# Each 1024-column scan run as two of 512 columns, one per channel block

## What is computed

```python
delta = softplus(dlt @ W_dt.T + b_dt)                       # (L, 1024)
A = -exp(A_log)                                             # (1024, 16)
deltaA = exp(delta[..., None] * A)
deltaBx = delta[..., None] * Bm[:, :, None, :] * xc[..., None]
def step(h, inp):                                           # over the positions
    dA, dBx, c = inp
    h = dA * h + dBx
    return (h, einsum('bdn,bn->bd', h, c))
y = (ys + xc * D) * silu(z)
out = y @ W_out.T
```

## Time and profile before

| what | value |
|---|---|
| median of 3 runs | 5346.54 us |
| lowest and highest | 5343.88 and 5351.52 us |
| span of the profiled execution | 5344.5 us |
| first scan to last scan | 136.8 to 3693.0 us |
| feed-forward part | from about 3700 us |
| DVE, PE, POOL, ACT busy over the span | 91%, 90%, 73%, 66% |

### The profile page before, as it was taken

One profiled execution on the slowest core, in us unless ns is written; L12 is line 12 of the kernel. 1 busy time (PEld: TensorE's weight loads), 2 busy tenths in 40 slices (PEclk: granted clock), 3 DMA queues, 4 the chain that ended last, 5 costly groups with the idle time before them and its releaser, 6 DMA issues. The chain is left out here.

```text
span 5344.5 us, 78097 instructions
## 1 busy us (share of the span) xinstructions
PE 4819.1 (90%) x21964; PEld 3313.7 (62%) x21964; DVE 4883.6 (91%) x4117; ACT 3542.1 (66%) x7757; POOL 3924.5 (73%) x1818
## 2 busy tenths in 40 slices
PE   8789898898988988889898898877999999999999
PEld 3455555555555555555555555555788888888888
DVE  7999999999999999999999999997788888888887
ACT  3777878778788787877877778765444444444442
POOL 5999999999999999999999999997222322223221
PEclk9899999999999999999999999988999999999999
DMA  7555565655555555555555555555001010110100
GB/s 249 173 187 186 179 197 175 190 190 173 192 177 194 190 172 192 179 188 183 185 190 175 192 184 180 184 167 185 27 31 33 29 35 29 31 33 29 35 29 28
DMA packets 402710, 745.76 MB, mean 140 GB/s; under 512 B 44083, under 2 KB 44211, under 8 KB 402198
## 3 DMA queue, kind: packets, MB, share of 16 engines
q1 hardware_dynamic: 401590, 738.08, 42.4%
q0 software_dynamic: 736, 3.41, 0.2%
HBM read 698.05 MB, written 43.26 MB: 139 GB/s over the span
## 5 line engine op out<-in xcount | busy, mean ns | idle before, releaser
L739 POOL TENSOR_TENSOR slot<-du,b_row 128x1024 f32<-128x1024 f32 x1024 | 2396.3, 2363 | 23.6 <-issue 15.5
L1119 DVE TENSOR_TENSOR_SCAN decays<-decays,state,slot 128x1024 f32<-128x1024 f32 x656 | 1539.0, 2346 | 59.1 <-ACT slot L970 58.3
L961 ACT ACTIVATE decays<-delta,rate 128x512 f32<-128x512 f32 x2048 | 1326.9, 679 | 23.8
L1250 PEld LDWEIGHTS y_ps<-ident,slot 128*128 128x128 f32 x8192 | 969.9, 146 | 336.5 <-issue 221.3
L1250 PE MATMUL y_ps<-ident,slot 128*128 128x128 f32 x8192 | 1058.2, 281 | 101.0 <-POOL slot L746 76.4
L1175 PE MATMUL work_ps<-h_t,win 128*128 128x512 f32 x2048 | 962.9, 614 | 83.9 <-ACT zs L839 34.7
L746 POOL TENSOR_TENSOR slot<-slot,c_row 128x1024 f32<-128x1024 f32 x368 | 868.6, 2360 | 131.6 <-ACT state L948 125.4
L1640 POOL TENSOR_TENSOR hq<-hid,qinv 128x1408 f32<-128x1408 f32 x63 | 163.3, 2593 | 1029.9 <-DVE qinv L1666 1029.9
L1119 DVE TENSOR_TENSOR_SCAN slot<-decays,state,slot 128x1024 f32<-128x1024 f32 x368 | 857.2, 2339 | 26.0 <-ACT slot L970 25.9
L1125 DVE TENSOR_TENSOR slot<-decays,c_row 128x1024 f32<-128x1024 f32 x656 | 801.9, 1222 | 54.5 <-DVE decays L1119 0.5
L1175 PEld LDWEIGHTS work_ps<-h_t,win 128*128 128x128 f32 x2048 | 385.9, 196 | 531.8 <-issue 431.2
(11 more groups left out here) (283 smaller groups left out, 7980.9 us busy)
## 6 DMA issues: line engine op xcount, KB each, us to landing
b_row<-b_c_rows SPq DMA_DIRECT2D x1024, 256.0 KB, 3.9
c_row<-b_c_rows SPq DMA_DIRECT2D x1024, 256.0 KB, 3.7
win<-in_w_in SPq DMA_DIRECT2D x256, 256.0 KB, 4.3
xt<-in_x SPq DMA_DIRECT2D x16, 1024.0 KB, 7.4
xr<-in_x SPq DMA_DIRECT2D x64, 256.0 KB, 4.1
x_after_mamba<-xr SPq DMA_DIRECT2D x64, 256.0 KB, 4.3
xa<-x_after_mamba SPq DMA_DIRECT2D x64, 256.0 KB, 2.8
xres<-x_after_mamba SPq DMA_DIRECT2D x64, 256.0 KB, 2.7
```

The lines of the kernel that those rows point to most:

```text
L739: pool.tensor_tensor(slot[:, u % SLOTS, :, :], du[:, p % 2, :, :], two(b_row[:, u % BC_RING, :]), ALU.mult).then_inc(S["ub_ready"], 1)
L961: act.activation(decay[u % 2][:, i, :], delta[:, p % 2, i, :], ACT.Exp, scale=rate[:, 2 * p + i, n:n + 1]).then_inc(S["decay_ready"], 1)
L1119: dve.tensor_tensor_scan(d if u in DVE_C else h, d, h, state[:, 2 * p, n:n + 1], ALU.mult, ALU.add).then_inc(S["scan_done"], 1)
L1250: op = pe.matmul(y_ps[i][:, s, :], slot[:, u % SLOTS, i, s * P:(s + 1) * P], ident[:, :], is_transpose=True, start=False, stop=(n == N - 1 ...
```

## The change

The scan, the C product on VectorE, the decays and the saving of states go by half units (one channel block each); the seam steps (`lead_exp`, `lead_mul`, `lead_in`) and their three buffers and five semaphores are gone. 41 units stay in `DVE_C`, but some are others: 1, 10, 16, 48 and 57 leave, 3, 15, 49, 55 and 58 come in. The step tables and `BANK` are new, with most steps moved by a position or two. GpSimd's B and C products stay 1024 wide. The diff, with the tables cut:

```diff
-                    def save_states(u, c):
+                    def save_state(u, i, c):
                         p, n = divmod(u, N)
-                        h = decay[u % 2] if u in DVE_C else slot[:, u % SLOTS, :, :]
                         if u in DVE_C:
-                            wait(act, *c_done(u, c))
-                        else:
-                            wait(act, S["scan_done"], c.at(UNITS, u + 1))
-                        act.activation(state[:, 2 * p:2 * p + 2, n], h[:, :, T - 1], ACT.Copy).then_inc(S["state_saved"], 1)
+                            wait(act, *((S["half_used"], half_used(u, c)) if i == 0 else c_done(u, c)))
+                            act.activation(state[:, 2 * p + i, n:n + 1], decay[u % 2][:, i, T - 1:T], ACT.Copy).then_inc(S["state_saved"], 1)
+                        elif i == 0:
+                            wait(act, S["scan_done"], c.at(2 * UNITS, 2 * u + 2))
+                            act.activation(state[:, 2 * p:2 * p + 2, n], slot[:, u % SLOTS, :, T - 1], ACT.Copy).then_inc(S["state_saved"], 2)
...
+                    def decays(u, i, c):
...
                         if n == 0:
-                            wait(act, *piece_read("d", 2 * p + 1, c))
-                            wait(act, S["lead_cut"], c.at(PAIRS, p + 1))
+                            wait(act, *piece_read("d", 2 * p + i, c))
                         if exists(cc) and v in DVE_C:
-                            wait(act, S["state_saved"], c.at(UNITS, u - 1))
-                        for i in (1, 0):
-                            act.activation(decay[u % 2][:, i, :], delta[:, p % 2, i, :], ACT.Exp,
-                                           scale=rate[:, 2 * p + i, n:n + 1]).then_inc(S["decay_ready"], 1)
-                    def lead_in(u, c):
-                        p, n = divmod(u, N)
-                        first = slot[:, u % SLOTS, 1, 0:1]
-                        if n == 0:
-                            wait(act, S["lead_ready"], c.at(PAIRS, p + 1))
-                        wait(act, S["ub_ready"], c.at(UNITS, u + 1))
-                        act.activation(first, first, ACT.Identity, bias=lead[:, p % 2, n:n + 1]).then_inc(S["u_led"], 1)
+                            wait(act, S["state_saved"], c.at(2 * UNITS, 2 * (u - 2) + i + 1))
+                        act.activation(decay[u % 2][:, i, :], delta[:, p % 2, i, :], ACT.Exp,
+                                       scale=rate[:, 2 * p + i, n:n + 1]).then_inc(S["decay_ready"], 1)
...
-                    def scan(u, c):
+                    def scan(u, i, c):
...
-                        wait(dve, S["decay_ready"], c.at(2 * UNITS, 2 * u + 2))
-                        wait(dve, S["u_led"], c.at(UNITS, u + 1))
-                        d, h = flat(decay[u % 2][:, :, :]), flat(slot[:, u % SLOTS, :, :])
-                        dve.tensor_tensor_scan(d if u in DVE_C else h, d, h, state[:, 2 * p, n:n + 1],
+                        wait(dve, S["decay_ready"], c.at(2 * UNITS, 2 * u + i + 1))
+                        if i == 0:
+                            wait(dve, S["ub_ready"], c.at(UNITS, u + 1))
+                        d, h = decay[u % 2][:, i, :], slot[:, u % SLOTS, i, :]
+                        dve.tensor_tensor_scan(d if u in DVE_C else h, d, h, state[:, 2 * p + i, n:n + 1],
                                                ALU.mult, ALU.add).then_inc(S["scan_done"], 1)
-                    def times_c(u, c):
-                        wait(dve, *ring_loaded(c_loaded, c, u))
-                        wait(dve, S["scan_done"], c.at(UNITS, u + 1))
-                        dve.tensor_tensor(slot[:, u % SLOTS, :, :], decay[u % 2][:, :, :], two(c_row[:, u % BC_RING, :]),
-                                          ALU.mult).then_inc(c_row_used[u % BC_RING], 1)
+                    def times_c(u, i, c):
+                        if i == 0:
+                            wait(dve, *ring_loaded(c_loaded, c, u))
+                        wait(dve, S["scan_done"], c.at(2 * UNITS, 2 * u + i + 1))
+                        op = dve.tensor_tensor(slot[:, u % SLOTS, i, :], decay[u % 2][:, i, :], c_row[:, u % BC_RING, :], ALU.mult)
...
-                                scan(pos, c)
+                                scan(pos, 0, c)
+                                scan(pos, 1, c)
...
-                                times_c(pos, c)
+                                times_c(pos, 0, c)
+                                times_c(pos, 1, c)
```

More of the change, by code:

```diff
@@ L32 @@
 BANK = {
[7 rows of a table removed]
[6 rows of a table added]
 }
 PE_STEPS = {
[11 rows of a table removed]
[11 rows of a table added]
 }
 ACT_STEPS = {
[L56 to L65, removed]
@@ L71 @@
[L71 to L74, removed]
+    0: [("sp_ln", 2, 0)], 1: [("z_out", 4, 0), ("ln_sum", 2, 1)], 2: [("y_out", 6, -1)],
+    4: [("sp_exp", 3, 0), ("y_out", 7, -1)], 5: [("sp_ln", 3, 0), ("z_out", 5, 0), ("xd", 0, 0)],
@@ new lines @@
+    6: [("ln_sum", 3, 1), ("ln_square", 0, 1)], 7: [("ln_square", 1, 1), ("ln_square", 2, 1)], 8: [("xd", 3, 0)],
+    9: [("z_out", 6, 0), ("ln_square", 3, 1), ("seed", 0, 1)], 12: [("residual", 0, -1)],
+    13: [("z_out", 7, 0), ("ln_apply", 0, 1)], 14: [("ln_apply", 1, 1)], 15: [("sp_exp", 4, 0), ("residual", 1, -1)],
+    17: [("sp_ln", 4, 0), ("ln_apply", 2, 1), ("xd", 2, 0)], 18: [("y_out", 1, 0)],
+    19: [("sp_exp", 5, 0), ("y_out", 0, 0)], 20: [("sp_ln", 5, 0), ("residual", 2, -1)], 21: [("silu_z", 0, 0)],
@@ new lines @@
+    22: [("ln_apply", 3, 1)], 23: [("h_out", 2, 1), ("xd", 5, 0)], 24: [("h_out", 0, 1)], 25: [("residual", 3, -1)],
+    26: [("h_out", 3, 1), ("h_out", 1, 1)], 28: [("in_out", 0, 1)], 29: [("in_out", 1, 1)], 30: [("conv_out", 0, 1)],
+    31: [("sp_exp", 6, 0), ("conv_out", 1, 1)], 32: [("sp_ln", 6, 0)], 33: [("in_out", 2, 1)],
+    34: [("y_out", 2, 0), ("xd", 4, 0), ("y_out", 3, 0)], 36: [("in_out", 3, 1)], 37: [("conv_out", 2, 1)],
+    39: [("in_out", 4, 1), ("sp_exp", 7, 0)], 40: [("conv_out", 3, 1), ("xd", 7, 0)], 42: [("in_out", 5, 1)],
@@ new lines @@
+    43: [("sp_ln", 7, 0)], 44: [("conv_out", 4, 1)], 45: [("conv_out", 5, 1)], 46: [("in_out", 6, 1)],
+    47: [("conv_out", 6, 1)], 50: [("in_out", 7, 1), ("xd", 6, 0)], 51: [("y_out", 4, 0)],
+    52: [("conv_out", 7, 1), ("y_out", 5, 0)], 53: [("silu_x", 0, 1)], 55: [("ln_sum", 0, 2)],
+    56: [("xd", 1, 1), ("x_out", 0, 1), ("z_out", 0, 1)], 57: [("sp_exp", 0, 1)],
+    58: [("sp_ln", 0, 1), ("z_out", 1, 1)], 59: [("z_out", 2, 1)], 60: [("sp_exp", 1, 1)], 61: [("sp_ln", 1, 1)],
+    63: [("sp_exp", 2, 1), ("ln_sum", 1, 2), ("z_out", 3, 1)],
@@ L534, in last_pieces, with half_used @@
                 return {BANK[ka]: ka for ka in order}
+            def half_used(u, c):
+                return c.at(len(DVE_C), sum(v <= u for v in DVE_C))
             def c_done(u, c):
                 return c_row_used[u % BC_RING], c.at(UNITS // BC_RING, u // BC_RING + 1)
[L540 to L541 removed]
             def two(row):
@@ L743, in times_c @@
                         h = slot[:, u % SLOTS, :, :]
-                        wait(pool, S["state_saved"], c.at(UNITS, u + 1))
+                        wait(pool, S["state_saved"], c.at(2 * UNITS, 2 * u + 2))
                         wait(pool, *ring_loaded(c_loaded, c, u))
@@ L951, in decays @@
+                    def decays(u, i, c):
                         p, n = divmod(u, N)
+                        v, cc = back(c, u - 2)
+                        if u == 0 and i == 0 and c.reg is None and c.off == 0:
+                            act.wait_ge(prep_rounded, len(PREP))
                         if n == 0:
-                            wait(act, *piece_read("d", 2 * p + 1, c))
-                            wait(act, S["lead_cut"], c.at(PAIRS, p + 1))
-                        v, cc = back(c, u - 2)
+                            wait(act, *piece_read("d", 2 * p + i, c))
@@ L974, in body @@
                             v, cc = back(c, pos - 2)
-                            if exists(cc) and (exists(c) or pos < 2):
-                                save_states(v, cc)
-                            if exists(c):
-                                decays(pos, c)
-                                lead_in(pos, c)
+                            saving = exists(cc) and (exists(c) or pos < 2)
+                            for i in range(2):
+                                if saving:
+                                    save_state(v, i, cc)
+                                if exists(c):
+                                    decays(pos, i, c)
                             for step, arg, cc in steps(ACT_STEPS, c, pos):
```

78 lines of the change are left out of this document (28 added, 50 removed), and 35 rows, old and new, of tables (BANK, PE_STEPS).

## The result

The changed kernel takes 5398.98 us (median of 4 runs, 5397.32 to 5400.36), the kernel before 5349.03 us (median of 4). The ratio is 1.0097, with a 95% interval of 1.0082 to 1.0111: 50 us slower, where 13 us faster were forecast. The profiled span grew from 5344.5 to 5396.4 us, 51.9 us.

The account below looks back on a forecast made before the run. VectorE and GpSimd were taken as nearly full, with chunks differing by VectorE's idle time. Terms 113 + 26 - 100 - 52 = -13 us took the 5344.5 us span to 5331.5 us; range 5275 to 5395.

Parts of the forecast that it names:

- A: VectorE's scans in halves, 1024 units: a half's pace 1.18 us, +113 us in all, bounds 46 and 126.
- Rival 1: A half scan's fixed part is at the top and ScalarE's stalls mostly stay: +45, 5390 us; chance 0.22.
- B: VectorE's C products in halves, 656 of them: 0.04 us more each, +26 us, bounds 13 and 39.
- C: VectorE's product no longer directly behind its own scan: 0.195 us goes at 32 places in each of 16 chunks, -100 us.
- D: Scans' stalls on VectorE shrink, behind silu steps (-34 us) and at chunk ends: -52 us in sum, bounds -20 and -75.
- Rival 2: It cancels: the silu stalls shrink (-34 us) but the chunk ends stay: +5, about 5350 us; chance 0.22.
- E: The rest, savings on ScalarE and moved steps in the queues of GpSimd, SP and TensorE: costed at nothing.
- Rival 4: Each VectorE instruction starts only when the one before has ended, so halves pay full duration: 5634 us; chance 0.03.

Follow-up runs that it names:

- e3: The changed kernel with VectorE's C product whole again, 1024 columns, behind both half scans: 5444.94 us, ratio 1.0180.
- e1: The changed kernel with the step tables, BANK and DVE_C of the kernel before, less the seam steps: 5339.51 us, ratio 0.9984.
- e12: e6 (changed kernel, z3 ahead of d2) with ScalarE's xd(0) moved back from position 5 to 0: 5337.17 us, ratio 0.9984.
- e11: e1 (halves, old lists) with TensorE's d2 ahead of z3, both at position 59: 5363.44 us, ratio 1.0035.
- e6: The changed kernel with one swap in TensorE's list at position 59, z3 ahead of d2: 5362.96 us, ratio 1.0030.
- e2: The kernel before, whole scans, with the changed kernel's PE, ACT, DVE and SP tables, BANK and DVE_C; seam steps and GpSimd's table unmoved: 5460.29 us, ratio 1.0213.

## Why the prediction was wrong, point by point

**A held.** The pace of a half scan was taken as 1.18 us and is 1.18 (durations 1272 and 1265 ns, of which 1240 to 1280 were given). The upper bound, from one operation at two widths, was nearly right. Rival 1 (+45) came close to the measured +50, but by luck: 26 of its 45 us are dearer halves, which were not paid. That only 20 us go off the scans' waits was nearly so in sum (16), but for the reordering and not for the reason that it gives.

**B held.** Two half products take 1.19 us against 1.18 taken. **C held.** The idle time before the products is gone, and e3 brought 46 us back where 57 were worked out. A, B and C together were forecast at +39 and came to 39.9.

**D was right behind the silu steps** (1.51 to 0.75 behind `silu_x` and to nothing behind `silu_z` in the chunk shown; 1.5 to between 0.36 and 0.48, and to nothing, in e1) **and wrong at the chunk ends of the changed kernel.** There -18 us stood in the sum, and the end grew instead. The size itself held where the lists allowed it: the scans wait 37 us in e1 and 33 in e12, and 33 was the forecast. Rival 2 had the ends stay as they were, and didn't go far enough either.

**E is the step that failed.** It saw that `z3` now stands behind `d2`, which waits for `sp_out(1)`, and counted nothing, "since its reader `z_out(3)` stays at position 63". That is no cover. In these rows the head of TensorE's queue, waiting, holds back what stands behind it, and the reader's position only says when the reader begins to wait: `d2` started at 1710.28, `z3` took 6.38 us more, and ScalarE was at `z_out(3)` at 1713.7. The price was 24 to 36 us (e11, e6). What D credited to `z2` ahead of `d1` was the same kind of step, read only where it helped. The move of `xd(0)` from position 0 to 5, more than the "position or two" of the text ahead, was not priced at all, though the first sum of a chunk and everything behind it on TensorE needs it: 26 us (e12). Forecast: -13, with nothing counted for these two. Measured: -9 with both put back (e12), -9 with all the old lists (e1), and +50 as the kernel stands. So the halves were priced right to some 4 us, and the whole miss is the reordering.

**The rule about the pipe.** Rival 4 falls: half scans of 1265 to 1272 ns follow one another after 1.18 us, and e3's waiting products cost 46 us. By the Trainium skill's rule that a semaphore costs nothing extra (VectorE: DVE Perf Modes, section The DRAIN you can't avoid) that wait would be free, and the trace disagrees. The same section adds that a next operation that is not held starts earlier, which the prediction left out; with that the trace agrees. The skill's half throughput of a scan (DVE: opcode table, instruction layouts, handler registers and perf-mode slots, section Datapath and trigger behaviour) agrees with the trace: 2346 ns at 1024 columns less 1272 at 512 is 1074 for 512 columns, 2.10 ns each, about twice the 1.041 of the prediction's part A.

**What stays open.** e12 gave 26 us where 11 to 18 were expected; against e6 the gate waits 20 us less and the scans 4, and the last 2 were not followed. What ScalarE waits for at every second chunk end is not known, and so neither is how much of the swap's price is due to it. Why the new lists cost 59 us with halves (the changed kernel against e1) and 111 with whole scans (e2) was read only from the waits at L968.

## What to carry to other kernels

When a diff changes instructions and also reorders the queues, price the reordering item by item: for each item that moved, what it waits for, what is queued behind it on its engine, and who waits for that. Splitting an instruction can give much of its cost back where its consumer is next in the same queue, since the second half covers the first half's latency: here the halves cost 139 us by the forecast's count and 40 net, and it was the shorter stalls that made e1 faster. Idle time in front of an instruction is no room for more work there if it is waiting for an input.

## What the runs showed of the hardware

TensorE's wait cost more than its length. The windows of the changed kernel during the 7.72 us wait, in the z matmul right behind it, and in the next z matmul (length, busy times, then granted clock, DMA share, GB/s):

```profile
1702.56:1710.28 7.72, 0.00 (x1) 0.00 (x0) 7.72 (x11) 5.87 (x14) 6.24 (x3) 0.74 0.34 117
1710.88:1717.26 6.38, 6.38 (x11) 2.67 (x10) 5.86 (x7) 2.56 (x5) 4.80 (x3) 0.56 0.52 174
1719.71:1723.31 3.60, 3.60 (x12) 1.64 (x11) 3.60 (x6) 1.62 (x4) 3.60 (x3) 1.00 0.18 36
```

Eight z matmuls take 6.38 us at a granted clock of 0.56, near the lower of the two levels (1.2 GHz), after TensorE had done nothing for 7.72 us; the next eight, of the same shape, take 3.60 us at full clock (2.4 GHz). So 2.8 us of `z3`'s lateness are the clock, on top of the wait for `d2`. I had priced no wait on TensorE this way.
